# Attention with W0 folded into the v weights and one ring of four PSUM buffers, q and k rounded to half precision by GpSimd

## What is computed

```python
h = _L0_tok_ref(x, ...)                       # conv of signs, 3 taps, 128 -> 64, batch norm
h = h + _L0_attn_ref(_layernorm(h), ...)
h = h + _L0_ffn_ref(_layernorm(h), ...)
# attention: B, N, D, H = 4, 748, 64, 8
qkv = x @ Wqkv + bqkv
q, k, v = jnp.reshape(qkv, (3, b, n, d, h))
score = jnp.einsum('bnqh,btqh->bnth', q, k) * d ** (-0.5)
attn = jax.nn.softmax(score, axis=1)
av = jnp.einsum('bnnh,bnqh->bnqh', attn, v)
out = av.reshape(b, n, d * h) @ W0 + b0
# ffn: each token walks a binary tree of 8 levels (score = x . w1s[node]),
# out = sum over the levels of gelu(|score|) * (x @ w2s[node] + b2s[node])
```

## Time and profile before

| | us |
|---|---|
| median of 3 runs (548.09 to 549.48) | 549.22 |
| the profiled execution | 548.32 |
| its span, first to last instruction | 546.5 |
| busy: PE, DVE, ACT, POOL | 378.2, 366.0, 299.8, 277.4 |

### The profile page before, as it was taken

One profiled execution on the slowest core, in us unless ns is written; L12 is line 12 of the kernel. 1 busy time (PEld: TensorE's weight loads), 2 busy tenths in 40 slices (PEclk: granted clock), 3 DMA queues, 4 the chain that ended last, 5 costly groups with the idle time before them and its releaser, 6 DMA issues.

```text
span 546.5 us, 8746 instructions
## 1 busy us (share of the span) xinstructions
PE 378.2 (69%) x3014; PEld 251.9 (46%) x3014; DVE 366.0 (67%) x594; ACT 299.8 (55%) x655; POOL 277.4 (51%) x315
## 2 busy tenths in 40 slices
PE   1333859888898988988588993556109996587780
PEld 1222525444465645655355651554007774354450
DVE  0644495878867789687888788625956999443341
ACT  2463767999888998889588694002001110254440
POOL 1456594322236287362677506838375777741211
PEclk9999996999999999999799996655558999599996
DMA  5202497397330333302331300750014110200000
GB/s 130 65 1 54 114 229 150 86 196 131 86 86 14 73 86 86 86 22 65 85 85 34 86 1 4 129 84 4 16 35 109 40 43 22 73 9 5 7 5 7
DMA packets 52029, 36.03 MB, mean 66 GB/s; under 512 B 25122, under 2 KB 50687, under 8 KB 51980
## 3 DMA queue, kind: packets, MB, share of 16 engines
q1 hardware_dynamic: 48238, 32.47, 27.4%
q0 software_dynamic: 2944, 2.45, 1.7%
q10 hardware_dynamic: 800, 0.49, 0.4%
HBM read 10.57 MB, written 8.79 MB: 35 GB/s over the span
## 4 chain that ended last, share of the span: by engine, by line
ACT 29%; PE 26%; DVE 25%; issue 8%; POOL 6%; DMA 3%; ACTq 0%; SPq 0%; POOLq 0%; DVEq 0%
ACT S L943 15%; PE S L735 5%; DVE nm L1097 5%; PE U L674 5%; DVE lm L1268 4%; DVE vT L1261 3%; ACT q L930 3%; ACT vT L930 3%; PE S L838 3%; ACT k L930 3%; DMA par<-in_L_tok_moving_var 2%; PE U L838 2%; POOL pool_a L459 2%; PE S L840 1%; POOL w L452 1%
## 5 line engine op out<-in xcount | busy, mean ns | idle before, releaser
L1097 DVE TENSOR_REDUCE nm<-S 128x1 f32<-128x748 f32 x192 | 171.9, 932 | 44.7 <-PE S L735 41.9
L943 ACT ACTIVATE S<-S,nm 128x748 f32<-128x748 f32 x192 | 167.1, 885 | 42.6 <-DVE nm L1097 41.4
L735 PE MATMUL S<-pool_a 128*128 128x512 f16 (+1 forms) x768 | 151.6, 332 | 29.6 <-ACT S L943 27.1
L735 PEld LDWEIGHTS S<-pool_a 128*128 128x128 f16 x768 | 68.9, 105 | 91.7 <-ACT S L943 56.2
L550 POOL DMA_INDIRECT out<-lm,vT x44 | 43.4, 985 | 58.1 <-DVE lm L1274 51.1
L459 POOL TENSOR_TENSOR pool_a<-q,pool_a 128x750 f16<-128x750 f32 x16 | 25.8, 1613 | 72.3 <-DVE pool_a L1064 72.1
L635 PE MATMUL U<-xhT,wq 128*128 128x250 f16 x288 | 42.9, 289 | 17.7 <-ACT q L930 8.2
L1268 DVE TENSOR_REDUCE lm<-vT 128x64 f32<-128x512 f32 x44 | 45.1, 1026 | 1.6 <-DVE vT L1261 0.5
L943 ACT ACTIVATION_READ_ACCUMULATOR S<-S,nm 128x1 f32 x192 | 44.0, 229 | 0.0
L635 PEld LDWEIGHTS U<-xhT,wq 128*128 128x128 f16 x288 | 27.1, 104 | 35.5 <-ACT q L930 13.7
L491 POOL DMA_INDIRECT sorted_rows<-xrow,slot x24 | 26.9, 1119 | 18.4 <-DVE slot L1183 10.3
(11 more groups left out here) (214 smaller groups left out, 681.6 us busy)
## 6 DMA issues: line engine op xcount, KB each, us to landing
pool_a<-pool_a SPq DMA_DIRECT2D x64, 187.5 KB, 3.0
pool_a<-pool_a SPq DMA_DIRECT2D x64, 93.8 KB, 2.8
sorted_rows<-zrow SPq DMA_DIRECT2D x1, 3864.0 KB, 22.3
vT<-sorted_rows SPq DMA_DIRECT2D x11, 276.0 KB, 3.7
w<-in_L_ffn_w2s SPq DMA_DIRECT2D x1, 2048.0 KB
lm<-in_x SPq DMA_DIRECT2D x4, 375.0 KB
pool_a<-in_L_ffn_w2s SPq DMA_DIRECT2D x1, 1024.0 KB
out<-lm,vT POOLq DMA_INDIRECT x44, 2.1
```

Source lines behind the costliest of these rows:

```text
L735: last = mm(S[n % 3][:, c0:c1], kst[:, u % 3, a, hd, START[t]:START[t] + P], qst[:, u % 3, hd, c0:c1], start=(a == 0), stop=(a == 1))
L943: sc_.activation(S[n % 3][:, 0:N], S[n % 3][:, 0:N], ACT.Exp, bias=nm[:, b % 2, j, i:i + 1], accum_out=sm[:, b % 2, j, i:i + 1]).then_inc( ...
L1097: v.tensor_reduce(nm[:, b % 2, j, i:i + 1], S[n % 3][:, 0:N], X, ALU.max, negate=True).then_inc(s_max, 1)
```

## The change

Edits, by place:

- PSUM: S and U become one ring Z of four buffers. Every fill (scores, projections, transposes, products) takes the next buffer in program order (`zone`), and TensorE waits until the fill four before it has been taken (`take`). `fills` writes down the order.
- v is not projected. The v weights of each head are multiplied by W0 once (`wt`, `wm`, units 0 and 1), rounded and split, and `heads_out` computes v W0 of a pair of heads for 125 tokens by 128 outputs, six tiles. `weigh_heads` (VectorE) multiplies by the softmax weights, `add_heads` (GpSimd) adds both heads to the residual rows. The product with W0, the broadcasts and `diag_scale` go.
- Softmax weights are made in each unit for the unit before (`diag_shift`, `diag_exp`, `diag_weights`).
- Score tiles have 125 rows (tokens in three classes modulo 3), so q, k are stored without a stride, and h goes through DRAM to be put in that order (`h_out`, `h_in`, 35 DMAs on SyncE).
- Rounding of q and k is done in `part_lo` on GpSimd; `hi_cast` on VectorE goes. SyncE may send the high parts of q before the low ones are there.
- The start: layer-norm groups are cut so that q and k of batch 0 need one group only; x of batches 2 and 3 is loaded later.

```diff
...
-        S = [ctx.enter_context(nc.psum_tensor(f"S{i}", [P, 1024], f32)) for i in range(3)]
-        U = ctx.enter_context(nc.psum_tensor("U", [P, 1024], f32))
-        U_D = 1000
+        Z = [ctx.enter_context(nc.psum_tensor(f"Z{i}", [P, 1024], f32)) for i in range(4)]
...
+        FIRST = [("q", 0), ("k", 0), ("q", 1), ("k", 1), ("xb", 2), ("xb", 3), ("xh", 1), ("cv", 2)]
+
+        def fills(u, i):
+
+            b, ph = u // NPAIR - 1, u % NPAIR
+            f = []
+            if 1 <= u <= NU and i == 0:
+                f.append(("d", u - 1))
+            if u + AHEAD < NU and i in (1, 3):
+                f.append(("qk"[i // 2], u + AHEAD))
+            f += {(0, 4): [("xh", 2)], (0, 5): [("cv", 3)], (0, 7): [("wt", 0)], (0, 9): [("wm", 0)],
+                  (0, 11): [("wt", 1)], (1, 2): [("wm", 1)], (1, 4): [("xh", 3)], (1, 5): [("wt", 2)],
+                  (1, 7): [("wm", 2)], (1, 9): [("cb", 0)], (1, 11): [("w1", 0)], (2, 5): [("y", 0)],
+                  (2, 9): [("y", 1)]}.get((u, i), [])
+            if 3 <= u <= NU and i == 5:
+                f.append(("y", u - 1))
+            if b >= 0 and ph == 2:
+                f += {5: [("t", b)], 8: [("l", b, 0)], 10: [("l", b, 1)]}.get(i, [])
+            if b >= 1 and (ph == 3 if b < B - 1 else ph == 1) and i == 7:
+                f.append(("r", b - 1))
+            if b == B - 1 and ph == 3 and i == 11:
+                f.append(("r", b))
+            return f
+
...
+        def act_takes(u, i):
+
+            u, i = (u, i + 1) if i < 2 * NT - 1 else (u + 1, 0)
+            return [f for f in fills(u, i) if f[0] in BY_ACT]
+
+        def dve_takes(u, i):
+
+            u, i = (u, i - 1) if i else (u - 1, 2 * NT - 1)
+            return [f for f in fills(u, i) if f[0] not in BY_ACT] if u >= 0 else []
...
+        def full(f):
+
+            return s_full, number[f] + 1
+
+        def zone(f):
+
+            return Z[(number[f] + 3) % 4]
...
             def part_lo(kind, w):
                 n = "qk".index(kind)
                 c = w % 2
+                pool.wait_ge(*freed[kind, w])
+                if w >= 2:
+                    pool.wait_ge(s_st[(w - 2) % 3], 16 * 8 * ((w - 2) // 3 + 1))
+                gp.tensor_copy(hl[:, c, n, 0, 0:N], (q32, k32)[n][:, c, 0:N]).then_inc((s_qc, s_kc)[n], 1)
                 pool.wait_ge((s_qc, s_kc)[n], w + 1)
-                gp.tensor_tensor(hl[:, c, n, 1, 0:QN], (q32, k32)[n][:, c, 0:QN], hl[:, c, n, 0, 0:QN],
+                gp.tensor_tensor(hl[:, c, n, 1, 0:N], (q32, k32)[n][:, c, 0:N], hl[:, c, n, 0, 0:N],
                                  ALU.subtract).then_inc(s_lo, 1)
...
+            def add_heads(w):
+                b = w // NPAIR
+                pool.wait_ge(s_wyv, w + 1)
+                if w % NPAIR == 0:
+                    pool.wait_ge(s_hb, b + 1)
+                hv = xrow[0:XP, b * NT:(b + 1) * NT, C_H:C_ID]
+                pw = prod[0:XP, w % 2]
+                link(gp.tensor_tensor(hv, hv, pw[:, :, 0, :], ALU.add))
+                gp.tensor_tensor(hv, hv, pw[:, :, 1, :], ALU.add).then_inc(s_hy, 1)
+                pool.wait_ge(s_hy, w + 1)
 
...
             part_lo("q", 0)
             part_lo("k", 0)
+            part_lo("q", 1)
+            part_lo("k", 1)
+            rstd1(1)
+            x_lo(1)
+            qk_prod(0)
+            qk_prod(1)
+            rstd1(2)
             x_lo(2)
-            x_lo(3)
-            qk_prod(0)
-            qk_lo(1)
-            for b in range(B):
-                h_bias(b)
-            token_numbers()
+            link(gp.memset(xrow[:, :, C_H:C_ID], 0.0))
+            pool.sem_inc(s_id, 1)
             for u in range(NU + NPAIR):
                 b, ph = u // NPAIR - 1, u % NPAIR
+                if u == 1:
+                    rstd1(3)
+                    x_lo(3)
                 if u + AHEAD < NU:
                     qk_lo(u + AHEAD)
+                if u == 1:
+                    token_numbers()
+                if u == 2:
+                    h_bias(0)
+                    h_bias(1)
+                    h_bias(2)
+                    h_bias(3)
+                    add_heads(0)
+                    add_heads(1)
+                if 3 <= u < NU:
+                    add_heads(u - 1)
...
+            def take(f):
+
+                if number[f] >= 4:
+                    pe.wait_ge(*freed[order[number[f] - 4]])
+                return zone(f)
+
...
+            def heads_out(w):
+
+                b, j = divmod(w, NPAIR)
+                z = take(("y", w))
+                if w == 0:
+                    pe.wait_ge(*freed["wm", 2])
+                    pe.wait_ge(s_cb, 1)
+                    pe.wait_ge(s_id, 2)
+                pe.wait_ge(*xhat_ready(GROUPS_FOR["v"][b]))
+                js = slice(j * P, (j + 1) * P)
+                for t in range(NT):
+                    r0, g = v_tile(b, t)
+                    zt = z[0:XP, t * P:(t + 1) * P]
+                    for a in range(2):
+                        mm(zt, xhT[:, r0:r0 + XP], mw[:, a, g * H * D + j * P:g * H * D + (j + 1) * P],
+                           start=(a == 0), stop=False)
+                    last = mm(zt, pick[:, g, 0:XP], cb[:, js], start=False, stop=True)
+                last.then_inc(s_full, 1)
...
-            def hi_cast(kind, w):
-                n = "qk".index(kind)
-                dve.wait_ge(s_ue, unit_no[(kind, w, 0)] + 1)
-                if w >= 2:
-                    dve.wait_ge(s_st[(w - 2) % 3], 16 * 8 * ((w - 2) // 3 + 1))
-                v.tensor_copy(hl[:, w % 2, n, 0, 0:QN], (q32, k32)[n][:, w % 2, 0:QN]).then_inc((s_qc, s_kc)[n], 1)
...
+            def diag_shift(w):
+
+                dve.wait_ge(s_max, 2 * NT * (w + 1))
+                dve.wait_ge(*full(("d", w)))
+                v.tensor_tensor(at[0:XP, w % 4], zone(("d", w))[0:XP, 0:2 * NT], nm[0:XP, w % 4],
+                                ALU.add).then_inc(s_dd, 1)
+                dve.wait_ge(s_dd, w + 1)
+                dve.sem_inc(s_fd, 1)
+
+            def diag_weights(w):
+
+                dve.wait_ge(*freed["s", w, 2 * NT - 1])
+                link(v.reciprocal(sm[0:XP, w % 4], sm[0:XP, w % 4]))
+                dve.wait_ge(s_ex, w + 1)
+                v.tensor_tensor(at[0:XP, w % 4], at[0:XP, w % 4], sm[0:XP, w % 4], ALU.mult).then_inc(s_at, 1)
+
+            def weigh_heads(w):
+
+                dve.wait_ge(s_at, w + 1)
+                dve.wait_ge(*full(("y", w)))
+                if w >= 2:
+                    dve.wait_ge(s_hy, w - 1)
+                av = at[0:XP, w % 4].rearrange("p (a t) -> p t a", a=2).unsqueeze(3).to_broadcast([XP, NT, 2, D])
+                v.tensor_tensor(prod[0:XP, w % 2], zone(("y", w))[0:XP, 0:NT * P].rearrange(
+                    "p (t a o) -> p t a o", t=NT, a=2), av, ALU.mult).then_inc(s_wyv, 1)
+                dve.wait_ge(s_wyv, w + 1)
+                dve.sem_inc(s_fd, 1)
+
...
+            center(0, Z[1])
             normalise(0)
...
+            center(1, Z[1][:, 512:1024])
+            signs(2)
+            signs(3)
+            normalise(1)
+            center(2, zone(("cv", 2)))
             normalise(2)
```

878 lines of the change are left out of this document (465 added, 413 removed).

## The result

The changed kernel takes 581.20 us (median of 4, 579.54 to 582.21) where the kernel before takes 548.88 in the same comparison: a ratio of 1.0587, 95% interval 1.0557 to 1.0616. The forecast was 519 us in a range of 500 to 541. The profiled execution spans 578.8 us. Some executions of a kernel take longer than its others at a lower granted clock, whatever the edit; the ratios and their intervals leave out those more than 1.5% above the shortest of the same kernel, and the medians do not.

A forecast was written before the change was run, and what follows sets the result against it. The prediction took plain units to be bound by ScalarE and, after the change, by ScalarE and VectorE level at 13.0 us. Gains of 4.9 (start), 15.1 (loop) and 10.5 (tail), 30.5 off 549.22, gave 519 us, range 500 to 541.

The forecast's parts named there:

- plain units of 14.2: Main loop: an ordinary unit falls from 14.74 to 14.2 us, with ScalarE and VectorE needing 13.0 each; 14 units, 198.8.
- the 8.5 us of lateness: Main loop: added for GpSimd late by 2.5 and 4.0 us, plus two for unit 3, where the first heads wait for `h_bias`.
- up to 15.7: Upper bound of a plain unit, from following one unit whose scores 7 to 9 stand behind the fill `y`; lower bound 13.05.
- Rival 2, the ring: Main loop: the shared ring costs more, units of 15.7, kernel 533 us; chance 0.15.
- The rival that ended slower: GpSimd's queue bounds the whole loop; slower from 2.7 us a cast, 561 us at 3.3; chance 0.07.
- Units 0 and 1: 38: First two loop units, with one-time work: together 38 us, from 39.7, losing v copies, gaining a layer-norm group, transposes and V-weights.
- GpSimd late by 2.5 and 4.0 us: Loop units 10 and 14: VectorE waits for GpSimd's sums, with casts taken at 1.2 us, by 2.5 and 4.0 us.
- VectorE 13.0 with its waits: Plain unit: VectorE, busy 11.64 before, needs 13.0 us including handovers of 0.4 and a wait for GpSimd of about 0.5.
- the ranks: Units 11 and 15 keep the ranks on VectorE: 6.1 us more than a plain unit each, 12.2 in all.
- the start, 56: Before the loop: first exponential at 56 us, 4.9 earlier, most of the early q's gain queued away; bounds 52 and 60.
- the tail 46.2: After the loop: 10.5 us won, to 46.2; x-hat of the last batch starts at 20.3, behind GpSimd's queue.
- the lock of 0.5 a unit: VectorE instruction with two SBUF operands (`at<-at,sm`) waits while GpSimd's instruction runs: about 0.5 us a plain unit.

The follow-up runs named there:

- y_merged: Changed kernel with one bias matmul of 256 columns for two tiles and weights 128 columns wide in the y fill, 15 matmuls for 18; 585.4 us, 1.006 of the kernel before.
- spread: Changed kernel with the q, k and y fills at steps 2, 5 and 8, not 1, 3 and 5; 604.9 us, 1.048 of the kernel before.
- best_hi: best without the product with the low half of v·W0, 9 matmuls a y fill; 586.6 us, 1.018 of the kernel before.
- best: Changed kernel with the edits of y_merged, spread and slots_late together; 563.2 us, 1.025 of the kernel before.
- y_w128: Changed kernel with y fill weights 128 columns wide instead of 125; 575.3 us, 1.045 of the kernel before.
- group 3: Kernels run together on one slower chip, beside the kernel before: the changed kernel again and edits of the places of its fills; the unedited one took 607.5 us there.
- y_nobias: Changed kernel without the bias matmul of each tile of the y fill, 12 matmuls for 18, bias of v missing from the output; 555.2 us.
- slots_late: Changed kernel with GpSimd's six row writes of batch 0 moved from the start of unit 12 to behind the sums of unit 13; 580.6 us, 1.062 of the kernel before.
- after_ref: The changed kernel once more, unedited, on the chip of group 3; 607.5 us, 1.052 of the kernel before.

## Why the prediction was wrong

**The failed step: plain units of 14.2.** "TensorE loses the v projection and the W0 product and gains 18 small matmuls; it was busy 12.02. So two engines need 13.0 each". The 18 got no price, and TensorE was left out of the chain. The six plain units shown above last 18.20 on average, 4.0 over the forecast; over 14 units that is 56 of the 63 us that the loop is too long (with the 9 of units 0 and 1 it is 65, and of the 8.5 us of lateness in the forecast most did not come). Of the 4.0, 3.15 are there at full clock (17.35), and 0.85 goes with the lower clock. Of the 3.15, 2.73 are the y fill, since a unit less its fill is 14.6 us in all five kernels with these places, and 0.4 is a rest that the runs do not take apart (moving q, k and y to steps 2, 5 and 8 takes 0.5 off). Without the fill the forecast of 14.2 would have been near.

How the fill does it is shown: it begins when exponential 3 is through, takes 2.73 us, 2.0 of them for the six bias matmuls, and then the next score and its maxima take 1.80, which alone use up the two exponentials of 0.86 us in store. The prediction followed a unit to "up to 15.7" and so saw the place, but counted the order of the buffers and not the time of the fill. Rival 2, the ring, pointed the right way with 533; no case reached 581. The rival that ended slower named GpSimd's queue, and GpSimd was busy 192.9 of the loop's 327.2 us, not over 9 tenths from unit 6 to 14 as forecast (only unit 8 has that, 16.96 of 18.13).

**The clock** had no term at all. The earlier trace rows had 1.00 in most units, and the forecast took that for granted. Its part is open. In units 2 to 15 there are 67 and 80 us at half clock in two profiles of the changed kernel, 34 with fills of 1.53 us (y_merged), 27 and 28 with fills of 0.75 and 0.40, which points at the fill; but spread has 44 with a fill of 2.68, best_hi 47 with one of 1.20 and best 27 with one of 1.54, and each of these has one profile. What makes the clock fall the runs do not show.

The weight loads play a smaller part. One of 128 columns takes 0.105 us on average in the changed kernel (L741), one of 125 columns 0.145 (L794) and 0.156 (L838); the kernel before had no half-precision load of 125 columns, so no row of it could warn. The Trainium skill, "TensorE: Matmul & The Clock Gate", section "Weight-path perf modes — Fast Weight Load (FWL) and DoubleRow", says that the fast load is on when the number of weights is 128 and the type is not single precision. The trace agrees with its direction, and y_w128 puts the price at 0.47 us a fill, 0.44 us a unit. The loads of the scores grew too, from 0.102 us in unit 3 before to 0.137 in unit 9 of group 3, but two scores take 1.43 us in both, so that cost nothing there; and in y_nobias 12 matmuls with such loads take 0.063 us each, less than one load. It is not chiefly the loads of 125 columns that make the fill long, but the bias matmuls between them.

**Units 0 and 1: 38** was 47.0. TensorE is busy 19.67 of 25.39 in unit 0, at PEclk 0.66; the transposes and products for v·W0 stand there. 9 us, mis-sized; in five other profiles, with the long unit 1, it is 53 to 55.

**GpSimd late by 2.5 and 4.0 us** in units 10 and 14: no such wait in unit 10, and 3.06 in unit 14. The cast took 0.81 and 0.83 us, not 1.2, inside the bounds of 0.65 and 2.13. The estimate of 0.6 from the Trainium skill, "GPSIMD Engine Reference", section 4.1, by roughly line rate with one input, was nearer, 0.2 too low. And units of 18 us gave GpSimd time: where they are shorter, the wait in unit 14 grows (6.4 us in y_nobias). That it is the row writes in unit 12 was shown by slots_late.

**Right, or near:** ScalarE 13.05 (13.1) in a plain unit, and VectorE 13.0 with its waits (busy 11.8 to 13.4); the ranks, 6.1 more in unit 11 (6.0 over 18.20); the start, 56 (53.63); the tail 46.2 (48.34), where x-hat of the last batch starts 21.8 us after the last exponential, for 20.3, released by GpSimd's queue; the feed-forward part 149.65 (149.60); the lock of 0.5 a unit, of which `at<-at,sm` shows 0.3 (467 ns on average, 0.17 us in unit 8).

## What to carry to other kernels

Price each fill of a shared ring by its own time on the producer, and follow it to the consumer: what the consumers have in store must cover the fill, the next score and its maxima together. Here two exponentials of 0.86 us barely covered the last two, and the fill, 0.40 as well as 2.73 us, came on top in full. An engine that is busy 12 of 14.7 us is no cover for that. And read the price of a matmul where it stands, not as a mean over the fill: 12 products took 0.75 us, and six more matmuls on 35 rows between them another 2.0. And where two changes come as one, try each alone: the half that looked dangerous was the half that paid.

## What the runs showed of the hardware

- Twelve half-precision matmuls of 128 columns, each with a weight load of its own of 128 rows by 125 columns, take 0.063 us each (0.75 together, y_nobias). Six more, with weights on 35 rows, one behind each two, make it 2.73 us (after_ref): 0.33 us for each. Three with 256 columns, and all weights 128 columns wide, make it 1.53 (y_merged).
- Weights 128 columns wide in place of 125 took 0.47 us off the fill of 18 (2.73 to 2.26), and nothing off the scores, where a load grew from 0.102 to 0.137 us and two scores took 1.43 us either way.
- The granted clock fell to half for 3.4 us at the end of a fill in which TensorE had no gap, and unit 1, with the same instructions but for one kernel, ran at PEclk 1.00 in ten profiles and at 0.71 to 0.75 in five.
- A cast of 748 elements from single to half precision takes GpSimd 0.81 us, against 0.29 for 128.
- The same kernel, before, took 548 to 549 us in three comparisons and 577 to 579 in the three others, on other chips; its twin with the rounding moved spent 232 and 231 us behind the loop there, against 206 for the kernel before on the first chip.
